# Sorting the first 352 tiles of edges on the chip by destination and source block, so that their source rows come from a table in SBUF instead of a gather

## The reference, cut to what matters

```python
dst = jnp.minimum((3125 * uniform(100000) ** 2.0).astype(int32), 49999)   # many edges at low dst
_o = jnp.argsort(dst); src = src[_o]; dst = dst[_o]                       # edges come sorted by dst
...
h = jnp.maximum(_layernorm(x), 0.0)
m_in = jnp.concatenate([h[src], h[dst], edge_attr], axis=1)               # edge_attr: one number an edge
msg = jax.nn.relu(m_in @ msg_w1 + msg_b1) @ msg_w2 + msg_b2
agg = segment_sum(msg, dst)
upd = jax.nn.relu(concatenate([h, agg]) @ upd_w1 + upd_b1) @ upd_w2 + upd_b2
x = x + h + upd
```

## Time and profile before

| | |
|---|---|
| median of three runs | 3720.36 us (3706.24 to 3729.26) |
| the profiled execution | 3713.86 us, its span 3712.0 us |
| granted TensorE clock over the span | 0.955 of full |
| PE busy | 3293.6 us (89%) |
| DVE, ACT, POOL busy | 1527.7 (41%), 1228.5 (33%), 852.0 us (23%) |
| edge phase, start to end | 2688.2 to 3695.5 us |

### The profile page before, as it was taken

The page is one execution under the profiler, slowest core; times in us unless marked ns, Lnnn a source line. Parts: engine busy times, 40 slices in busy tenths (PEclk is TensorE's granted clock), DMA queues, the critical chain, the costliest instruction groups (busy, mean ns, idle before and its releaser), DMA issues. The chain is left out here.

```text
span 3712.0 us, 88060 instructions
## 1 busy us (share of the span) xinstructions
PE 3293.6 (89%) x23372; PEld 2394.6 (65%) x23373; DVE 1527.7 (41%) x4456; ACT 1228.5 (33%) x3858; POOL 852.0 (23%) x928
## 2 busy tenths in 40 slices
PE   5989998999998899997899999999877787878887
PEld 3666666667753444444799999998745555555555
DVE  7877778889810400004432121113322333333333
ACT  6766777777710400004332221123311111111111
POOL 2000000000020000000000000001277777777775
PEclk8999999999999999997999999999888999899989
DMA  3011222333377398890343222224233333333332
GB/s 67 18 51 65 72 77 94 103 115 109 120 186 185 87 232 188 187 236 26 102 123 91 77 77 77 77 74 120 62 83 78 80 79 78 80 77 79 78 78 71
DMA packets 118671, 367.64 MB, mean 99 GB/s; under 512 B 32905, under 2 KB 74359, under 8 KB 105765
## 3 DMA queue, kind: packets, MB, share of 16 engines
q1 hardware_dynamic: 89572, 310.74, 31.0%
q0 software_dynamic: 25664, 51.90, 6.2%
q10 hardware_dynamic: 3154, 1.60, 0.2%
HBM read 280.52 MB, written 83.62 MB: 98 GB/s over the span
## 5 line engine op out<-in xcount | busy, mean ns | idle before, releaser
L2355 POOL DMA_INDIRECT edge_rows<-src_table,src_idx x784 | 757.4, 966 | 239.9 <-issue 238.6
L2499 ACT ACTIVATE edge_act<-edge_ps 128x512 f32<-128x512 f32 x196 | 117.0, 597 | 887.9 <-PE edge_ps L2457 887.9
L2471 PEld LDWEIGHTS edge_ps<-edge_hot,edge_act 128*128 128x128 f32 x1760 | 256.9, 220 | 157.5 <-issue 156.9
L2457 PE MATMUL edge_ps<-edge_rows,ident 128*128 128x512 f32 x392 | 261.6, 754 | 108.3 <-DMA edge_rows<-src_table,src_idx 107.5
L1197 PE MATMUL prop_ps<-rows,y 125*128 125x500 f32 (+1 forms) x798 | 306.5, 543 | 15.9 <-DMA rows<-adj_rows 9.1
L760 ACT ACTIVATE build_place<-build_place,w 128x128 f32<-128x128 bf16 x690 | 264.9, 402 | 142.0 <-DVE build_place L704 101.1
L830 PE MATMUL build_ps<-build_place 128*128 128x325 bf16 (+1 forms) x1380 | 299.0, 298 | 1.5 <-ACT build_place L760 0.3
L2471 PE MATMUL edge_ps<-edge_hot,edge_act 128*128 x1760 | 278.0, 308 | 6.4 <-issue 5.5
L2449 PE MATMUL edge_ps<-m_store,edge_hot_t 125*128 x2640 | 232.1, 230 | 56.2 <-issue 34.5
L822 PE MATMUL build_ps<-build_place 128*128 128x325 bf16 (+1 forms) x690 | 207.4, 301 | 65.9 <-DVE build_place L706 30.8
L704 DVE TENSOR_SCALAR build_place<-key_id,lane,one_w 128x128 f32<-128x128 f16 x690 | 237.1, 344 | 57.3 <-issue 28.4
(11 more groups left out here) (380 smaller groups left out, 5830.5 us busy)
## 6 DMA issues: line engine op xcount, KB each, us to landing
rows<-adj_rows SPq DMA_DIRECT2D x62, 1367.2 KB
cnt_panels<-build_cnt SPq DMA_DIRECT2D x50, 683.6 KB
adj_rows<-rows SPq DMA_DIRECT2D x25, 1367.2 KB
n<-cnt_panels SPq DMA_DIRECT2D x40, 683.6 KB
orders_panel<-cnt_panels SPq DMA_DIRECT2D x40, 683.6 KB
edge_dst_row<-dst_rows SPq DMA_DIRECT2D x196, 125.0 KB
h<-cnt_panels SPq DMA_DIRECT2D x20, 683.6 KB
edge_rows<-src_table,src_idx POOLq DMA_INDIRECT x784
```

What stands on the lines that cost most here:

```text
L2355: pool.indirect_dma_start(rows[s][:, i, :], None, dr.table, bass.IndirectOffsetOnAxis(ap=g.src_idx[:, t:t + 1], axis=0)).then_inc(s_rows[s ...
L2457: pe.matmul(ps[:, s, :], g.ident[:], rows[s][:].rearrange("p a k -> p (a k)"), start=False, stop=True, skip_group_check=True).then_inc(s_p ...
L2471: last = pe.matmul(bank, act[s][:, i, :], hot[:, bass.ds(here, 1), i * B:(i + 1) * B].rearrange("p a k -> p (a k)"), start=i == 0, stop=i ...
```

## The change

**What is computed stays the same**; the first SORTED = 352 tiles (45056 edges, dst up to 630, so six dst blocks) go another way.

1. class EdgeSort (in propagation_phase): a counting sort of those edges by (dst block, source block). Each of the 128 partitions holds 352 edges in order. DVE counts them in a histogram (50 instructions over 352 elements), PE turns the counts into start positions in four small steps that stand behind rows 4, 9, 11 and 13 of pass 0, and then, for each of the 25 source blocks, DVE makes a mask, a running sum (tensor_tensor_scan) and a predicated copy (352 elements each), with one ACT activation. The result is a position for each edge; a tile then holds edges of one dst block and one source block, padded with empty slots. 439 tiles come out for this data, in groups of 8 that never mix dst blocks: 59 groups (22, 10, 9, 7, 7 and 4), run as 60.
2. orders_phase: POOL starts with 352 indirect DMAs (L2288), each of which scatters 128 edges of 8 bytes to their places in a DRAM list. The weight loads stand behind them and behind the waits for TURNED. p and q are both kept in fp32 in SBUF (a3.pq); end_left and two ACT copies per end are gone.
3. edge_phase begins with a prologue: SP loads the list back (80 partitions of 16 KB), DVE and ACT make from it the lane within the source block, the dst numbers, the ranges of blocks and each tile's source block, SP stores these to DRAM and loads the ranges and source blocks back as tables, PE turns the dst numbers (16 transposes).
4. Then ROUNDS = 54 rounds of one sorted group and one gathered group, 8 tiles each, and 3 rounds of two sorted groups. The sorted group needs no gather: hot_s (126 x 1024, fp32, the source's one-hot, with ea as its last row) times the p table of the tile's source block, whose address comes from a register. Only 432 tiles are gathered. q is multiplied in fp32, one matmul a tile in place of three. Ranges are read from ranges, 2 registers for each group; the 8 source blocks by two loads of 4 registers. There are now 60 x 8 + 432 = 912 tiles where there were 784. The gathered groups touch 73 blocks in 54 groups, so 19 of them touch two. hot and hot_t now have one buffer for each of the two slots, and a hot is made only after the sums before it (s_sum n + 1, where it was n).
5. setup_phase: three small memsets on POOL and one DMA that fills the list with empty slots.

```diff
 class EdgeSort, new (propagation_phase, DVE)
+        for at in range(2 * NB):
+            v.tensor_scalar(self.unread[at % 4], self.both, float(at), None, ALU.is_equal, ALU.add,
+                            accum_out=self.hist[:, at // NB, at % NB:at % NB + 1]).then_inc(self.s_hist, 1)
...
+        def mask(s):
+            v.tensor_scalar(self.mask[s % 3], self.key, float(s), None, ALU.is_equal).then_inc(self.s_mask, 1)
+        def count(s):
+            v.tensor_tensor_scan(self.cum[s % 2], self.moved[s % 2], self.mask[s % 3], self.start[:, s:s + 1],
+                                 ALU.add, ALU.add).then_inc(self.s_cum, 1)
+        def place(s):
+            v.copy_predicated(self.pos, self.mask[s % 3], self.cum[s % 2]).then_inc(self.s_put, 1)
...
 orders_phase, POOL
+            for j in range(SORTED):
+                turn, lot = divmod(j // LOT, len(s_scattered))
+                if turn and j % LOT == 0:
+                    pool.wait_ge(s_scattered[lot], turn * LOT * 16)
+                pool.indirect_dma_start(dr.slots, bass.IndirectOffsetOnAxis(ap=g.src_idx[:, j:j + 1], axis=0),
+                                        g.pay[:, j, :], None).then_inc(s_scattered[lot], 16)
+            for sem in s_scattered:
+                pool.wait_ge(sem, SORTED // len(s_scattered) * 16)
+            pool.wait_ge(s_tr, TURNED)
...
 edge_phase, POOL
-                    pool.wait_ge(s_pre[s], r + 1)
-                    for i in range(GT):
-                        t = (r * SLOTS + s) * GT + i
+                if r:
+                    pool.wait_ge(s_rows, r * (16 * GT))
+                if r >= AHEAD:
+                    pool.wait_ge(s_pre[GATHERED], r - AHEAD + 2)
+                for i in range(GT):
+                    t = SORTED + r * GT + i
...
 edge_phase, DVE
+            do(v.tensor_reduce(blocks, words[:, :, :, 0], AX.X, ALU.max))
...
+            v.tensor_tensor(lane16[:], words[:, :, :, 0], bc(scaled, 128), ALU.add).then_inc(s_lanes, 1)
...
+            v.scalar_tensor_tensor(raw[:, :, :, 0], dst16[:], float(N), dst16[:], ALU.is_lt, ALU.mult).then_inc(s_dstf, 1)
...
+            def turned(r, s, wide):
+                load_range(v, regs, r, s)
+                if wide or s != GATHERED:
+                    v.wait_ge(s_src[s], r * 16 + (16 if s != GATHERED else 16 - 16 * ROUNDS))
+                    v.tensor_scalar(hot_s[s][0:B, :], src_row[s][:], lane[0:B, :], None, ALU.is_equal).then_inc(s_hot_s[s], 1)
+                lo, end = limits_of(v, regs, s)
+                with v.Fori(lo, end) as d:
+                    n = made[s].next()
+                    v.wait_ge(s_dst[s], r * 16 + 16)
+                    v.wait_ge(s_free[s], n)
+                    v.tensor_scalar(hot_t[s][:], dst_row[s][:], g.block_base[0:B, bass.ds(d, 1)], lane[0:B, :],
+                                    ALU.add, ALU.is_equal).then_inc(s_hot_t[s], 1)
...
-                    v.wait_ge(s_sum, n)
+                    v.wait_ge(s_sum, n + 1)
...
 edge_phase, PE
+                load_range(pe, regs, r, s)
+                if wide or s != GATHERED:
+                    group = r if not wide else r * 2 + (s - ROUNDS)
+                    for i in range(0, GT, 4):
+                        pe.load(tiles[i:i + 4], sources[0:1, bass.ds(group * GT + i, 4)])
...
+                def source(i):
+                    return pe.matmul(place(s, i), hot_s[s][:, i * 128:(i + 1) * 128],
+                                     a3.pq[0:B + 1, bass.ds(at[i], 1), 0, :].rearrange("p a k -> p (a k)"),
+                                     start=i % 4 == 0, stop=False, skip_group_check=True)
...
-                        for p in range(3):
-                            last = pe.matmul(ps[:, s, i * 128:(i + 1) * 128], hot_t[:, bass.ds(here, 1), i * 128:(i + 1) * 128]
-                                             .rearrange("p a k -> p (a k)"),
-                                             a3.q_parts[:, bass.ds(d, 1), p, :].rearrange("p a k -> p (a k)"),
-                                             start=False, stop=False, skip_group_check=True)
+                        last = pe.matmul(place(s, i), hot_t[s][:, i * 128:(i + 1) * 128],
+                                         a3.pq[0:B, bass.ds(d, 1), 1, :].rearrange("p a k -> p (a k)"),
+                                         start=False, stop=False, skip_group_check=True)
```

645 lines of the change are left out of this document (462 added, 183 removed).

## The result

| | before | after |
|---|---|---|
| median | 3719.41 us (3706.24 to 3729.26, 4 runs) | 3565.74 us (3552.05 to 3566.42, 4 runs) |
| ratio | | 0.9582, 95% interval 0.9558 to 0.9606 |
| span of the profiled execution, granted clock | 3712.0 us, 0.955 | 3564.7 us, 0.971 |
| start of the edge phase | 2688.2 us | 2700.5 us |
| first edge matmul of PE in it | 2693.5 us | 2733.2 us |

The kernel is 154 us faster, 4.2%. From the first edge matmul to the phase's end it takes 815 us, where it took 1002 and where I had predicted 986. The prologue came out as predicted (32.7 us against 32), and the stretch ahead of the phase took 12 us more, where I had said 0.

What follows compares the result with a forecast made beforehand. The prediction took gathers to bound the kernel before and PE the changed one. Edge phase -16, prologue +27 and the rest 0 made +11 us, taken as 3730 us, range 3625 to 3860.

Steps and rivals of the forecast that it cites:

- The prologue: Start of the edge phase: list back, DVE work, tables stored and reloaded, 32 us against 5.3, so +27 us.
- What bounds the kernel before: Edge phase before the change: POOL's gathers run without pause and are the bound, 784 x 1.25 = 980 us.
- The registers: PE's edge rounds: register loads leave 1.8 us open for the three loads and 0.5 for the rest, each round.
- a lead of 0.8: PE's sequencer in a mixed round: runs 0.8 us ahead during the static sums, hiding that much of 2.6 us.
- the loads of registers may hide wholly behind eight static sums: Rival on PE's edge rounds: loads hidden, clock perhaps held, 13.4 us a round, 3633 us in all; chance 22%.
- The matmuls: PE's mixed edge round at full clock: sorted group 5.7 us, gathered group 6.3, together 12.0 us.
- Two blocks: The 19 gathered groups touching two blocks: extra matmuls and waits for DVE, 6.9 us each, 131 us.
- The clock: PE in the edge phase: granted clock 0.93 or so, costing 5% of 750 us of matmuls, 37 us.
- the wide rounds: Three edge rounds of two sorted groups each: six groups of 7.6 us on PE, 46 us.
- Outside the edge phase: Sort, scatters, weight loads and unsplit p and q in the other phases: all together 0 us.
- The rival with the late cover: Sort or scatters overrun their cover: pass 1 late by 12 us, or POOL's weights by 170 us, 3900; chance 7%.
- POOL: Changed edge phase: POOL takes 13.4 us a round, starts four rounds ahead, isn't the bound; rival that it stays so: 5%.

Runs made afterwards that it cites:

- Experiment 1: The kernel before with POOL gathering only in its first round, later groups reusing those rows: 3568.41 us, ratio 0.9608.
- experiment 3: The changed kernel with register addresses for the sum matmuls (3888.36 us), or four (3665.12 us) or eight (3847.11 us) more register loads ahead of each sorted group.
- experiment 4: The changed kernel with gathers in the first four rounds only (3577.20 us), or with ten gathers a round instead of eight (3670.43 us).
- experiment 2: The kernel before without gathers after round one: two more used four-register loads a round on PE, 3607.19 us; PE's loop over pairs of rounds instead, 3561.65 us.

## Why the prediction was wrong, step by step

**What bounds the kernel before: right.** Experiment 1 confirms it: without the gathers it falls by 154 us.

**The registers: wrong, the largest error.** I charged 2.3 us a round for loads and control, 54 x 2.3 = 124 us, taking 1.8 of it from "2.6 less a lead of 0.8". The round of 11.47 us has nothing of it. The step that failed is the lead. The 2.6 came out near the truth: the sequencer needs 2.5 us from the sums to the first source. It did so by luck, since it was put together from loads of 1.3 us and 0.19 us a register, and a load of four registers takes 0.33 us (0.40 with what is between it and the next); what I read as its price in the earlier trace rows contained the branch back, 0.47, and half of the 2.5 us isn't loads. But the lead is 2.6 us and not 0.8, because the sequencer is through with the eight sums while PE is still at the identity, and so it covers all of the 2.5 (experiment 3). The prediction named this as a rival ("the loads of registers may hide wholly behind eight static sums") and gave it 22%; even that rival still had 13.4 us a round, and its 3633 us are 67 too many.

**The matmuls: slightly too dear.** 12.0 us predicted, 11.47 measured: a source matmul with an address costs 0.235 instead of 0.265, as does a static one, since the sequencer keeps ahead of it, and the identity takes 1.72 instead of 1.96. Together with the registers this is 54 x 2.8 = 151 us of the 171 by which the 986 was too long; nearly all of the other 20 is the clock (below).

**Two blocks: right.** 7.1 us each measured, 6.9 predicted.

**The clock: wrong.** I took 5% of the matmuls (37 us) by a line through the earlier trace rows from busy share to clock. The granted clock is 0.98, and what is left for it is less than half of the 37: 54 x 11.47 + 19 x 7.1 us and the 43 that the wide rounds took (I had 46) make 797 of the 815, and short waits are in the 18 too. These runs don't lie on such a line: 80% busy and 0.90 in the earlier trace rows, 77% and 0.89 with eleven loads (836.8 of 1090 us), but 78% and 0.96 with fp32 q and all gathers:

```profile
2700.00:3690.00 990.00, 768.88 (x4655) 550.44 (x4654) 339.52 (x653) 115.90 (x194) 746.53 (x770) 0.96 0.31 77
```

What settles it stays open.

**The prologue: right.** 32.7 us against 32.

**Outside the edge phase: 12 us where I said 0.** Setup and build take 2.6 us longer, propagation_phase 3.5 and query_key_phase 8.4; the orders phase takes 2.2 less. The 8.4 are the clock: PE is busy there throughout in both, and the level of 0.50 lasts for 40 us from its first matmul there (1714.3 us to about 1754) instead of 23 (1708.2 to about 1731). The start of the edge phase lies from 2679.6 to 2695.8 us in seven profiles of kernels of the old form (mean 2686.6), and from 2684.7 to 2709.9 in ten of the new one (mean 2696.5). So one profile can't settle a term of 10 us there; about 10 us more in the mean is what they show. And they don't lie where this pair has them: query_key_phase takes 83 to 97 us in kernels of both forms, short in four of the seven and in five of the ten, so that its 8.4 us are for the most part those of the execution profiled. propagation_phase takes 651 to 662 us in the old form (mean 657) and 659 to 676 in the new (mean 666), though its first pass, where the sort runs, ends only 2 us later in the mean. What the sort or its neighbours do to the later passes stays open. The sort fits its cover as predicted (its last copy ends at 1169.8 us, 1193.3 was the limit), and so do the scatters (1.28 us each, the last near 2240 us). The rival with the late cover falls.

**POOL: right for a reason that was thin.** POOL isn't the bound (experiment 4), but its round is 14.2 us, not 13.4, and it would have been the bound had PE's edge matmuls run without the stalls at second blocks. Nor was it four rounds ahead when PE began, as I had said: at 2733.22 us it is in its third round, which began at 2730.2.

## What to carry to other kernels

Price a register load, a branch or an address by what stands ahead of it: behind a run of matmuls with fixed addresses it is free up to the lead (2.6 us here), behind matmuls that each need an address there is little or no lead and it shows as idle time (0.40 us for each further load in experiment 2). Read the price of a load from the sequencer's own rows; a gap that holds several such things must be taken apart before it is multiplied. First ask which engine is the bound and what the time would be with that engine's work removed: that shows how much relieving it alone can give. Two engines within a few per cent of each other must be relieved together: fp32 q alone gave nothing, second buffers alone some 23 us, and with POOL's later wait 75.
